# All five hand-written instruction orders of a fused two-layer kernel laid out anew, piece by piece

## What is computed

```python
xn = layernorm(x)
x  = x + attention(xn)          # 16 query heads of 8, 4 key/value heads, softmax over 256 keys
       + gated_ffn(xn)          # top 2 of 8 gates, one shared relu FFN of 512: gate * (relu(xn@w1)@w2)
xn = layernorm(x)
x  = x + mamba_like(xn)         # in-projection to 512, 4-tap causal convolution, silu, softplus step,
                                # h = h*exp(-A*dt) + B over 16 states and 256 steps, gate, out-projection
       + ternary_ffn(xn)        # silu(xn@w1)*(xn@w2), two hidden 512x512 gelu layers, out-projection
```

## Time and profile before

| | us |
|---|---|
| Median of three runs | 371.86 |
| Lowest and highest run | 370.92, 372.0 |
| Span of the profiled execution, first to last instruction | 370.3 |
| PE busy | 361.6 (98%) |
| ACT busy | 314.4 (85%) |
| DVE busy | 303.1 (82%) |
| POOL busy | 238.0 (64%) |

### The profile page before, as it was taken

How to read it: one execution, slowest core, us unless ns; L and a number is a source line. 1 busy time by engine, 2 the same in 40 slices (tenths; PEclk the granted TensorE clock), 3 DMA queues, 4 the chain that set the end, 5 groups by cost and what they waited for, 6 DMA issues and landing times.

```text
span 370.3 us, 5874 instructions
## 1 busy us (share of the span) xinstructions
PE 361.6 (98%) x1810; PEld 185.9 (50%) x1810; DVE 303.1 (82%) x508; ACT 314.4 (85%) x540; POOL 238.0 (64%) x287
## 2 busy tenths in 40 slices
PE   7999999999999999999999999999999999999996
PEld 6757454546454553433324445465445464464546
DVE  4786879978788888579878768989999989998950
ACT  4934878886988887899998899999999999799870
POOL 2156504642527211342989673999999999999990
PEclk9999999999999999999969999999999999999999
DMA  6477282746265220220000000001000000000000
GB/s 217 125 145 147 93 200 35 174 143 120 58 110 123 43 55 2 52 85 0 1 21 3 1 0 2 0 0 48 5 0 21 0 3 28 1 2 1 0 28 28
DMA packets 29902, 19.63 MB, mean 53 GB/s; under 512 B 4496, under 2 KB 28848, under 8 KB 29616
## 3 DMA queue, kind: packets, MB, share of 16 engines
q1 hardware_dynamic: 29872, 19.26, 21.3%
HBM read 13.69 MB, written 5.37 MB: 51 GB/s over the span
## 4 chain that ended last, share of the span: by engine, by line
PE 68%; ACT 8%; DMA 2%; issue 2%; DVE 2%; SPq 0%; POOL 0%; ACTq 0%; DVEq 0%; POOLq 0%
PE bank L908 15%; PE bank L896 13%; PE bank L357 6%; PE bank L980 4%; PE bank L342 4%; ACT da L1088 3%; PE bank L869 3%; PE bank L885 3%; PE bank L886 3%; PE bank L953 3%; PE bank L933 3%; PE bank L388 2%; PE bank L328 2%; PE bank L396 2%; PE bank L970 2%; ACT pt L548 2%
## 5 line engine op out<-in xcount | busy, mean ns | idle before, releaser
L1218 POOL TENSOR_TENSOR acc<-acc,hb 128x512 f32<-128x512 f32 x128 | 158.1, 1273 | 11.6 <-DVE hb L1163 11.2
L1163 DVE TENSOR_TENSOR_SCAN hb<-da,bank 128x512 f32<-128x512 f32 x128 | 145.9, 1200 | 15.1 <-PE bank L869 9.1
L589 DVE TENSOR_REDUCE mx<-bank 128x2 f32<-128x512 f32 x128 | 83.1, 683 | 16.9 <-PE bank L328 14.4
L1088 ACT ACTIVATE da<-dt,nega 128x510 f32<-128x510 f32 x128 | 82.2, 713 | 0.2
L548 ACT ACTIVATE pt<-bank 128x512 f32<-128x512 f32 x128 | 71.2, 596 | 9.8 <-PE bank L342 8.7
L896 PE MATMUL bank<-sil,ld 128*128 128x512 f32 x128 | 59.1, 595 | 0.0
L908 PE MATMUL bank<-gelu,ld 128*128 128x512 f32 x128 | 58.5, 593 | 0.1
L342 PE MATMUL bank<-q_st,k_st 51*128 51x512 bf16 x128 | 42.2, 386 | 1.8 <-ACT pt L548 1.5
L328 PE MATMUL bank<-k_st,q_st 48*128 48x256 bf16 x240 | 38.9, 273 | 0.1
L896 PEld LDWEIGHTS bank<-sil,ld 128*128 128x128 f32 x128 | 24.3, 192 | 26.3 <-issue 25.7
L908 PEld LDWEIGHTS bank<-gelu,ld 128*128 128x128 f32 x128 | 23.8, 190 | 25.6 <-issue 24.7
(11 more groups left out here) (148 smaller groups left out, 534.0 us busy)
## 6 DMA issues: line engine op xcount, KB each, us to landing
q_st<-q_scr SPq DMA_DIRECT2D x8, 384.0 KB, 4.9
q_st<-q_scr SPq DMA_DIRECT2D x15, 192.0 KB, 3.8
ld<-in_pack SPq DMA_DIRECT2D x2, 1024.0 KB, 6.3
q_scr<-qk_parts SPq DMA_DIRECT2D x8, 192.0 KB, 2.1
k_st<-k_scr SPq DMA_DIRECT2D x15, 96.0 KB, 4.5
q_scr<-qk_parts SPq DMA_DIRECT2D x8, 128.0 KB, 2.1
out<-x SPq DMA_DIRECT2D x8, 128.0 KB, 1.9
ld<-in_pack SPq DMA_DIRECT2D x1, 968.0 KB, 5.4
```

The source lines that it names most:

```text
L589: eng.tensor_reduce(mx[:, 2 * pair:2 * pair + 2, q], s_bank[n % 2][:, :].rearrange("p (h k) -> p h k", h=2), AX.X, ALU.max).then_inc(mx_ok, 1)
L1088: act(da(n)[:, :, 1:T], dt[:, g % 2, c, :].rearrange("p (b n) -> p b n", b=GB)[:, :, 1:T], ACT.Exp, scale=nega[:, c, s:s + 1]).then_inc(da ...
L1163: eng.tensor_tensor_scan(hb[:, s % NPAIR, c, :], da(n).rearrange("p b n -> p (b n)"), b_bank(g, s)[:, :], 0.0, ALU.mult, ALU.add).then_inc ...
L1218: TT(acc[:, g % 2, c, :], acc[:, g % 2, c, :], hb[:, s % NPAIR, c, :], ALU.add).then_inc(add_ok, 1)
```

## The change

The pieces, their waits and their buffers are the same. Only the five strings of `ORDERS` are different, and the program has two more source lines, so that line 342 is line 344 after, and so on. One line of the diff each, of SP and of PE:

```diff
-    sync="""2*x_in head ffn_weights constants0 x_in 3*put fetch stack 3*put fetch stack 3*put 3*rows fetch loads 2*put
+    sync="""x_in head constants0 x_in ffn_weights x_in 3*put fetch 3*put fetch put stack put stack put 2*rows loads
-    tensor="""9*warm xn_transposes 4*warm project ffn_in v_gate 6*warm ffn_in 2*S warm xn_transposes S project ffn_out 2*S
+    tensor="""19*warm xn_transposes 3*warm project 2*warm ffn_in 2*warm v_gate ffn_in xn_transposes 2*S project 2*S
```

More of the change, by code:

```diff
@@ L72 @@
 ORDERS = dict(
-    sync="""2*x_in head ffn_weights constants0 x_in 3*put fetch stack 3*put fetch stack 3*put 3*rows fetch loads 2*put
-        rows put 2*rows loads stack fetch 3*rows stack 3*put fetch loads 3*rows 3*put fetch stack 3*rows 3*put fetch
-        stack 3*rows put stack 2*put fetch 3*rows stack 3*rows b_rows loads b_rows 2*out 2*b_rows 6*out landed""",
-    tensor="""9*warm xn_transposes 4*warm project ffn_in v_gate 6*warm ffn_in 2*S warm xn_transposes S project ffn_out 2*S
[L77 to L122, removed]
+    sync="""x_in head constants0 x_in ffn_weights x_in 3*put fetch 3*put fetch put stack put stack put 2*rows loads
+        rows fetch loads rows put 2*rows put stack put fetch loads put 3*rows stack 2*put fetch 2*rows loads rows
+        3*put fetch stack 3*rows 3*put fetch stack 3*rows 3*put stack fetch 5*rows stack rows 2*b_rows out b_rows out
+        b_rows 6*out landed""",
@@ new lines @@
+    vector="""ones moments inverse moments inverse first_split M v_out M moments 5*M gate_sum M gate_norm 2*M gated
+        6*M inverse 2*M v_out 4*M gate_sum 2*M gate_norm M clear M gated 15*M heads v_out 2*M gate_sum 3*M back_out
+        2*M residual 2*M gate_norm 4*M gated 2*M v_out 2*M heads 3*M back_out 3*M gate_sum residual 5*M gate_norm M
+        gated 2*M v_out 2*M heads 2*M gate_sum M back_out M gate_norm residual 4*M gated 8*M v_out 3*M gate_sum M
+        heads gate_norm back_out 2*M residual 4*M statistics 2*M gated M v_out 4*M heads 2*M gate_sum M gate_norm
+        back_out M inverse1 M residual gated 7*M v_out 3*M heads 2*M gate_sum 2*M back_out gate_norm M gated M
+        residual 2*conv mul 2*xm zm clear mul zm mul scan mul conv scan conv scan zm scan heads scan zm scan back_out
+        scan clear 3*scan residual scan heads scan back_out scan residual statistics scan inverse1 2*scan 2*conv 2*mul
+        2*zm scan 2*mul 9*scan 2*residual1 6*scan 2*conv scan 2*mul 2*zm 2*scan 2*mul 3*scan residual1 2*scan
+        residual1 11*scan mul scan mul scan 2*mul 8*scan residual1 3*scan 3*residual1""",
@@ L123 @@
+    gpsimd="""ones 2*biased G qk_split 7*G qk_split maxima_split 8*G biased qk_split maxima_split constants 6*G
+        maxima_split 2*G qk_split 5*G maxima_split 3*G qk_split 8*G maxima_split qk_split 8*G maxima_split qk_split
+        8*G maxima_split G shifted 7*G maxima_split start split start 5*add split 11*add start 10*add shifted 4*add
+        start add y add y start 7*add split 2*add start 22*add y add y 2*add start 8*add split 11*add start 10*add y
+        2*add y 31*add 2*y""",
 )
```

32 lines of the change are left out of this document (added).

## The result

The changed kernel takes 387.43 us (median of four runs, 386.37 to 389.27) against 371.49 us in the comparison's own runs of the kernel before (370.92 to 372.0). The ratio is 1.0433, with a 95% interval of 1.0403 to 1.0463: 15.9 us slower. The forecast was 378.7 us with a range up to 386.0, so the sign was right and the time lies 1.4 us outside the range. The profiled execution took 387.55 us for a span of 385.8.

A forecast was written before the change was run, and what follows sets the result against it. Layer 0 was taken as a lockstep of PE, ACT and DVE, with ACT and then PE full later. 2.5 + 3.1 + 1.8 = 7.4 us, less 0.6, gave 6.8 and 378.7 us; range 370.0 to 386.0.

The forecast's parts named there:

- The chain's members keep their places: Reordered pieces on DVE, POOL and the rest of PE: taken as 0, between -3 and +1.5 us.
- SP, batch 0: A's last rows DMA lands behind puts, two stacks and the first pack: 2.5 us later, between 0.1 and 3.5.
- SP, batch 2: Third pack issued at about 58 to 60 us, before the rows: costs 0, at most 0.5 us.
- SP, batch 3: Fourth pack issued ahead of the third rows, which land no sooner than it: A 3.1 us later, or 2.0.
- SP, batch 7: stack waits for the second rows, negation 1.5 us earlier: 1.8 us later, otherwise 3.3 or 0.9.
- PE, start: 38 warm matmuls delay the first transposes by 1.3 us, covered by batch 0's queue wait: 0, uncovered up to 1.3.
- ACT's tables: Three table loads fewer on ACT, 3.85 us, saved where PE is full: worth 0, between 0 and -0.5 us.
- give-back of 0.6 us: In layer 0 stalls let DVE and ACT catch up, so PE waits less: 0.6 us back, between 0 and 1.3.
- The clock falls in the stalls: Rival, chance 0.20: PE's new waits at 35 and 81 us bring half-rate stretches, 5.0 us more, 383.7 us.
- The small DMAs are not held up: Rival, chance 0.18: rows DMAs slip between a pack's pieces; 371.9 us, between 370.5 and 373.5.
- a faster order: Rival, chance 0.16: new order fills PE's waits in layer 0, winning 3.2 us with the queue costing nothing: 368.7 us.

The follow-up runs named there:

- tenth: Changed kernel with both stack pieces back behind their fetch and packs 0, 2 and 3 right behind the rows of batches 0, 2 and 3: 374.98 us.
- third run: Changed kernel with packs 0, 2 and 3 moved right behind the three rows of batches 0, 2 and 3; stack pieces left between the puts: 378.46 us.
- eleventh run: Changed kernel with only the stack pieces of batches 0 and 1 back behind their fetch, all packs as in the change: 384.20 us.
- second run: Kernel before with SP's new order alone, the other engines in their old orders: 389.14 us.
- ninth run: Changed kernel with SP's old order and POOL's constants moved back to batch 6: 379.73 us.
- eighth run: Changed kernel with 16 more warm pieces (32 matmuls on constants) on PE ahead of A at its first head of batch 0: 385.61 us.
- 6: Kernel before with PE, ACT, DVE and POOL in the new order from 152 us on, SP old throughout: 373.24 us.
- 12: Kernel before with PE, ACT, DVE and POOL in the new order only from 152 to about 197 us: 372.55 us.
- 13: Kernel of the tenth run with PE, ACT, DVE and POOL back in the old order behind 197 us: 374.26 us.
- seventh run: Changed kernel with SP's old order throughout and PE, ACT, DVE and POOL back in the old order from 158 us on: 376.87 us.
- the first: Changed kernel with SP's old order, the other four engines keeping their new orders: 378.21 us.
- the fifth: Changed kernel with SP's old order throughout and the other engines' old orders for pieces begun by 45 us in the trace before: 380.49 us.

## Why the prediction came out low

Three steps failed, and three terms were mis-sized. "The third [pack] is issued at about 58 to 60, before the `rows` of batch 2: 0, at most 0.5 us" failed: that place cost 2.4 us. The half-rate stretches behind the waits were no part of the sum: they cost 3.7 us. "The chain's members keep their places" failed: the other engines' orders cost about 1.9 us. Batch 0 was put at 2.5 us and cost 3.9, batch 3 at 3.1 and cost 3.6. Batch 7's 1.8 us didn't come; it was by luck that this error went against the others and left the time only 1.4 us outside the range.

The starts of `A` at the first heads of batches 0 to 7, from the timelines of five kernels:

| kernel | b0 | b1 | b2 | b3 | b4 | b7 |
|---|---|---|---|---|---|---|
| before | 35.02 | 49.02 | 64.66 | 81.00 | 97.61 | 149.73 |
| changed | 39.30 | 54.54 | 72.46 | 93.62 | 111.64 | 163.52 |
| 10: moves at batches 0, 2, 3 undone | 35.36 | 49.57 | 65.08 | 82.40 | 99.01 | 150.95 |
| 3: stacks alone stay | 38.83 | 54.07 | 69.56 | 86.94 | 103.58 | 155.54 |
| 11: packs alone stay | 37.50 | 51.50 | 69.57 | 90.62 | 108.64 | 160.52 |

Changed less tenth: 3.9, 5.0, 7.4, 11.2, 12.6 and 12.6 us. The gap is complete at batch 4 and neither grows nor shrinks behind it, which is why a wait in layer 0 costs its full length.

*SP, batch 0: forecast 2.5, found 3.9, and 1.0 more from the clock.* The mechanism, a small DMA that lands late behind large ones, was right; the term was too small and divided wrongly. My sum let the puts and stacks be through at 28.7 + 6.8 = 35.5 us and gave the pack the other 2.0. With the pack behind the `rows` (third run) `A` stood at 38.83, and the pack's place ahead of the third `rows` added only 0.5 us to that (39.30). So the term that was mis-sized is that of the two stacks, with the second pack's 282 GB/s for the first pack a smaller error beside it: from 28.0 to 39.3 us the queue moved 193 to 194 GB/s. The two costs also don't add: 3.5 and 2.1 us by themselves, 3.9 together. Why 1232 KB took longer than the 6.8 us that 182 GB/s gives stays open.

*SP, batch 2: forecast "0, at most 0.5", found 2.4, and 1.3 from the clock.* This step failed. `loads` waits for the landing of `fetch` of batch 3, which was issued at 59.89, and so the pack was issued at 64.97, 1.5 us ahead of the three `rows` at 66.50. It is tempting to put this down to the loss at batch 0, which moved the pack from the forecast's 58 or 60 us to 65 us. But that loss moved the `rows` as well. In the eleventh run, where the kernel is far less late at that point, the distance is the same (62.09 to 63.55), and so is the wait. In the tenth run `fetch` of batch 3 was issued at 55.22; with the 5.1 us that the pack waited behind it in the changed kernel it would have gone out at 60.3, still 1.2 us ahead of the `rows` at 61.53. What went wrong is that "before the `rows`" was taken for harmless, and the pack's 5.4 us of landing, which I had used at batch 3, was not used here: from 60 it gives 65.4, behind `A`'s 64.66, and the 208 KB of `put` that stand between pack and `rows` come on top. How far ahead a pack must be, the trace before could have told. It has its third pack ahead of the `rows` of batch 3, which I overlooked when I wrote that each stood on a queue with no pack ahead of it:

```profile
71.69 0.47 SPq L289 DMA_DIRECT2D ld<-in_pack  x1
```

That is 5.6 us ahead of the `rows` at 77.28, and these landed in 1.8 us. In the second run, with the old orders of the other engines, the new place at batch 2 cost 0.9 us only; why their new orders make it 2.4 is open.

*SP, batch 3: forecast 3.1, found 3.6, and 1.4 from the clock.* `max_rows` of batch 3 started at 84.33 in the changed kernel and at 75.68 in the tenth, 8.65 us apart, where batch 2's `A` was 7.4 apart: that is put down to batch 2's half-rate stretch, 1.3. Just behind it the tenth run loses 1.0 us at a `fetch` (0.6 of it marked as idle), and the changed one doesn't: 7.65. To 11.2 it is 3.6 for the wait. Right in mechanism and nearly in size: the pack landed after 5.8 us and the 8 KB behind it after 5.3.

*SP, batch 7: forecast 1.8, found 0.* The negation ended at 155.95 us, a shift of 10.1 where the kernel's was 14.4, so it came 4.3 us earlier and not 1.5. That covered two issues and `stack`. The second run, without that gain, shows 2.8 us. The mechanism stands; the cover was mis-sized.

*PE, start:* no cost beside the 0.3 us by which `A` of the tenth run is late. ACT's tables: 16 loads at line 1090 in place of 18, worth nothing here. The give-back of 0.6 us is not seen in the constant gap of 12.6.

*PE, ACT, DVE and POOL otherwise: forecast 0 (-3 to +1.5), found about 2.* The tenth run is 374.98 less 371.8, 3.2 us, slower than the kernel before. Not all of that is the other engines'. Of the 1.4 us by which its `A` of batch 3 is late, 1.0 is that wait for a `fetch`, and SP makes it: the tenth run's third pack and a `stack` stand right ahead of batch 4's last puts, for which this `fetch` waits. The last of these puts, issued at 67.58 us in the tenth run and at 67.52 us in the ninth, which has SP's old order, took to land:

```profile
k_scr<-qk_parts SPq DMA_DIRECT2D x1, 48.0 KB, 5.6
...
k_scr<-qk_parts SPq DMA_DIRECT2D x1, 48.0 KB, 2.8
```

The ninth run has no such wait and is 0.4 us late at 93 us. For the rest, the tenth run's shift is 2.1 us at `step_in`, falls to 0.1 us at 191 us as the half-rate stretch of the earlier trace rows is absent, and rises again at `third` and at the last `out`, to 2.9 us. I had argued that the chain's members keep their places; the end shows that they did not:

```profile
374.59 2.49 POOL L1228 TENSOR_TENSOR y<-acc,zs 128x512 f32<-128x512 f32 x2
```
```profile
377.34 2.02 PE L972 MATMUL bank<-wout_half,y 128*128 128x128 f32 x16 [1.35 <-POOL y L1228]
```

The earlier trace rows had PE arrive 0.35 us after POOL; now it arrives 1.35 us ahead of it. POOL's idle time before its additions rose from 11.6 to 16.7 us, 16.6 of it ended by DVE's scans.

*The rivals.* "The clock falls in the stalls" is what happened, beside the forecast's queue and not in its place: every one of the three waits was followed by half rate, for 3.4 us each and not 6.9, and with it went 1.0 to 1.4 us and not 2.5. (That the half rate is what costs them was tested at batch 0 alone, by the eighth run.) The second run, with the same SP order, has stretches of 6.8 us. I had made an addition to the forecast into an alternative with 0.20 of the chances. The rule of the Trainium skill ("TensorE: Matmul & The Clock Gate", part 1), that half rate is the resting state and activity lifts it, agrees with the eighth run. "The small DMAs are not held up" is refuted by landings of 4.1 to 5.3 us; "a faster order" by the tenth run.

So the 15.4 us by which the last `out` pieces are late (377.34 against 361.97) are 3.9 + 2.4 + 3.6 = 9.9 of waits for `rows` (the trace's own idle times make 9.6), 1.0 + 1.3 + 1.4 = 3.7 of half-rate stretches behind them, and 1.9 of the other engines' orders (the 2.9 by which the tenth run is late there, less the 1.0 of its `fetch`): 15.5. The forecast had 6.8 of it. What stays open is where the rest of the tenth run's 2.1 us in layer 0 arises. The gain of about 2 us at 185 us was taken back in layer 1 where the new order went on behind it (6, 10) and where the old one came back at 197 us (12, 13); the seventh run, with the old order from 158 us on, kept it to its end, from a start that was 5.6 us late. Why is open.

## What to carry to other kernels

When an edit puts a large DMA ahead of a small one on a queue, price the small one by its landing behind the large one, at every such place. That the large one is issued first doesn't clear it: here 5.6 us ahead was enough, and 0.6 to 1.5 us ahead was not. Look for the distance between the two in the new order, and not for the old time of either; a shift moves both. Add to each complete wait of PE the half-rate stretch that may stand behind it, as an addition to the forecast and not as a rival. And before orders of two versions are mixed to find a cause, look for pieces that wait for something only the other version has brought early: four of the thirteen runs (the first, the fifth, the seventh and the ninth) measured my mixture in part.
